# Attention and expert layer on one core: projected tiles, turned heads and the output projection change places between two PSUM banks

## The chip, the cores and the metric

The program runs on one core of a Trainium2 chip. The metric is the device time of one execution in microseconds (us), lower is better. The engines are named as in the profile: PE is TensorE (PEld its weight loads), DVE is VectorE, ACT is ScalarE, POOL is GpSimd, and SP issues most of the DMAs.

## The reference, cut to what matters

```
# x [32, 512, 256]; 16 heads of 16 channels
qk = x @ W_attn + b_attn;  q, k = halves;  v = x
y  = causal_attn(q, k, v)
e  = v[1:] - y[:-1];  k2 = x[:-1] @ W_k2 + b_k2
y2 = causal_attn(q[1:], k2, e), a row of zeros ahead
x  = layernorm(x + y @ W_proj + y2 @ W_proj + 2 * b_proj)
x  = layernorm(x + experts(x))    # eight experts, top 2
```

The arithmetic is float32; the scores come from three products of rounded and rest parts.

## The kernel before

**Units.** One batch element is eight units, called places 0 to 7: places 0 to 3 are the first attention for four groups of four heads, places 4 to 7 the second attention (`a` = 1) for the same groups. 32 batches make 256 units. A unit has ten slots. Every engine walks over the same range of times (unit x 10 + slot) and issues what is due at each; the order on each engine is therefore written out by hand, and engines meet only by semaphores.

**Scores, twice.** In each slot PE makes one bank of transposed scores of the present unit (line 714, into one of three banks `score_t`) and one bank of plain scores of the unit five ahead (`LEAD`, line 725, into one of three banks `score`). ACT takes the exponential of `score_t` (line 570), and POOL masks it on the diagonal (line 456). DVE takes the row maxima of `score` (line 932, two instructions each for most slots); these maxima are transposed on PE (line 793), negated on ACT (lines 604, 605) and sent by DMA into rows of `stack_q`, so that the later score matmul subtracts them. The two matmuls of a slot are issued alternately, and before them PE waits for both:

```
e.wait_ge(s_exp, now - KEY_DEPTH + 1)                             # depth 3
e.wait_ge(s_max, MAX_BEFORE[SLOTS] * u + MAX_BEFORE[n + 1])       # u, n: three slots back
```

So PE can be at most three slots ahead of DVE's maxima.

**Runs and gaps.** PE does the score slots in four runs: slots 0, 1, 2; slots 3, 4; slots 5, 6, 7; slots 8, 9 (`RUNS`). After each run there is a gap with other work:

- First gap (after slot 2): the weighted values of the unit before, key blocks 1, 3, 2 (`weigh`, line 675, into the bank `out_t`). ACT then copies `out_t` to `heads_t` (line 596).
- Second gap (slot 4): in places 1 and 2 the attention sum `y_sum` is transposed into the bank `misc` (line 747) for ACT's copy `y_t` (line 613). In every unit `heads_t` is turned back by four transposes into `out_t` (line 754); DVE divides it by the sums of the softmax (lines 946 and 952, below called the division).
- Third gap (slot 7): in places 7, 0, 1, 2, 4, 5 a projected tile of q, k or k2, six matmuls into `misc` (line 780, `PIECES`), which ACT copies out (`part_f`, line 582) and POOL splits (lines 484, 486). In places 3 and 6 half of the output projection of the batch before, eight matmuls into `misc` (line 810), which DVE adds to the residual (line 960). In places 3 and 7 one transpose of the maxima (line 793).
- Fourth gap (slot 9): the weighted values of key block 0 of this unit, into `out_t` (line 675).

**Following work.** `USUAL` names the unit and slot at which each step of the output projection and the layer norm of a batch is due, counted from the start of the next batch; `LAST` does so for the last batch. DVE's norm statistics (line 319) and the addition (line 960) are issued after the maxima of the slot that is named. POOL makes `value2` or the sum of both attentions (lines 523, 530) at slot 0 two units later. The expert layer starts in the last five units, in which no maxima are left to make, and ends the program.

The change touches the tables above, and the blocks for `ended`, `(place, slot)` and `due(...)` in the programs of all five engines.

Of the kernel before, what the change touches and what calls it, by code (L numbers as in the profile page):

```python
# [14 lines left out]
P = 128  # L15
# [33 lines left out]
PIECES = {(7, 7): ("k", 0, 0), (0, 7): ("q", 0, 1), (1, 7): ("k", 1, 2), (2, 7): ("q", 1, 3),  # L49
          (4, 7): ("k2", 0, 4), (5, 7): ("k2", 1, 5)}  # L50
# [7 lines left out]
USUAL = {"proj": ((3, 7), (6, 7)), "added": ((4, 0), (7, 0)), "stats": ((5, 5), (6, 4), (7, 5), (8, 1)),  # L58
         "var": ((8, 3),), "guess": ((8, 4),), "refine": ((8, 5),), "apply": ((8, 8), (11, 1), (11, 6), (12, 4)), "store": ((12, 7),)}
LAST = {"proj": ((3, 7), (4, 7)), "added": ((3, 9), (4, 9)), "stats": ((4, 1), (4, 3), (5, 1), (5, 2)),  # L60
        "var": ((5, 3),), "guess": ((5, 4),), "refine": ((5, 5),), "apply": ((5, 7), (5, 8), (5, 9), (6, 0)), "store": ((6, 1),)}
# [11 lines left out]
def build_layer(nc, x, x_turned, w_attn, b_qk, w_k2, w_proj, b_proj,  # L73
# [15 lines left out]
    with ctx:  # L89
# [242 lines left out]
        def _(e):  # L332
# [5 lines left out]
            for time in times:  # L338
# [20 lines left out]
                ended = time - 7  # L359
# [12 lines left out]
                if (place, slot) == (5, 5) and 2 <= b < batches:  # L372
# [55 lines left out]
        def _(e):  # L428
# [17 lines left out]
            for time in times:  # L446
# [28 lines left out]
                ended = time - 3  # L475
# [26 lines left out]
                if (place, slot) == (7, 2) and 0 <= ahead + 1 < batches:  # L502
# [12 lines left out]
                if slot == 0 and 0 <= done < end:  # L515
# [38 lines left out]
        def _(e):  # L554
# [4 lines left out]
            for time in times:  # L559
# [24 lines left out]
                ended = time - 7  # L584
# [4 lines left out]

                if slot == 2 and 0 <= unit - 1 < end:  # L590
                    e.wait_ge(s_pv, GROUP * unit)
                    if unit == 1:
                        e.wait_ge(s_floor, GROUP)
                    if unit >= 2:
                        e.wait_ge(s_turned, unit - 1)
                    e.activation(heads_t[:, :], out_t[:, :], ACT.Identity, bias=sum_floor[:, 0:1]).then_inc(s_heads, 1)  # L596
# [9 lines left out]

                for hf in range(halves):
# [53 lines left out]
        def _(e):  # L661
# [17 lines left out]
            for time in times:  # L679
# [56 lines left out]

                b = ahead - 1
                if 0 <= b < batches:
                    for hf in range(halves):
                        if (place, slot) == ((1, 4), (2, 4))[hf]:  # L740
                            e.wait_ge(s_full, min(N_PIECES * (b + 2) + 2 + hf, N_PIECES * batches))
                            if hf == 0:
                                e.wait_ge(s_added, GROUPS * (b + 1))
                            else:
                                e.wait_ge(s_yt, halves * b + 1)
                            for t in range(blocks):
                                done = e.transpose(misc[:, t * P:(t + 1) * P], y_sum[b % 2][:, t, hf * P:(hf + 1) * P], ident[:, :])  # L747
                            done.then_inc(s_yt_pe, 1)


                if slot == 4 and 0 <= unit - 1 < end:
                    e.wait_ge(s_heads, unit)
                    for t in range(blocks):
                        done = e.transpose(out_t[:, t * P:(t + 1) * P], heads_t[:, t * P:(t + 1) * P], ident[:, :])  # L754
                    done.then_inc(s_turned, 1)
# [3 lines left out]
                if piece:  # L759
# [7 lines left out]
                    if place == 1 and ahead >= 1:  # L767
                        e.wait_ge(s_yt, halves * ahead - 1)
                    if place == 2 and ahead >= 1:
                        e.wait_ge(s_yt, halves * ahead)  # L770
                    if place == 4 and ahead >= 1:
                        e.wait_ge(s_attended, 2 * ahead - 1)
                    if place == 7 and ahead + 1 >= 0:
                        e.wait_ge(s_negl, 2 * ahead + 3)
# [9 lines left out]
                for a, b in ((0, ahead + 1), (1, ahead)):  # L784
                    if (place, slot) == ((7, 2), (3, 2))[a] and 0 <= b < batches:
                        e.wait_ge(s_max, MAX_BEFORE[SLOTS] * (UNITS * b + GROUPS * (a + 1)))
                        e.wait_ge(s_full, min(N_PIECES * (b + 1) + (4 if a else 0), N_PIECES * batches))
                        if ahead >= 1:
                            if a:
                                e.wait_ge(s_yt, halves * ahead)  # L790
                            else:
                                e.wait_ge(s_attended, 2 * ahead)
                        e.transpose(misc[0:64, 0:P], max_cols[b % 2][:, a, :, :, :].rearrange("p s h q -> p (s h q)"),
                                    ident[:, :]).then_inc(s_neg_pe, 1)

                now_due = due("proj", time)
                if now_due:
# [4 lines left out]
                    e.wait_ge(s_full, min(N_PIECES * (b + 2) + (6 if pair else 4), N_PIECES * batches))  # L802
                    if pair:
                        e.wait_ge(s_attended, 2 * b + 1)
                    elif b + 1 < batches:
                        e.wait_ge(s_negl, 2 * b + 4)
                    for j in range(2):
                        t = 2 * pair + j
                        for c in range(halves):
                            done = e.matmul(misc[:, j * width:(j + 1) * width], y_t[:, c, t * P:(t + 1) * P], wp[:, c, :],  # L810
                                            start=(c == 0), stop=(c == halves - 1))
                    done.then_inc(s_proj, 1)


                if slot == 9 and 0 <= unit < end:
# [5 lines left out]
                    if unit:  # L821
                        e.wait_ge(s_normal, unit)
# [66 lines left out]
        def _(e):  # L889
# [27 lines left out]
            for time in times:  # L917
# [17 lines left out]
                if slot == 4 and 0 <= unit - 1 < end:  # L935
                    b, a, g = unit_parts(unit - 1)
                    heads = out_t[:, :].rearrange("p (t h w) -> p t h w", t=blocks, h=GROUP)
# [17 lines left out]
                if now_due:  # L955
# [4 lines left out]
                    e.tensor_tensor(rows2, misc[:, :].rearrange("p (t c) -> p t c", t=2), rows2, ALU.add).then_inc(s_attended, 1)  # L960
# [108 lines left out]
```

## Time and profile before

| | |
|---|---|
| median of 3 runs | 2380.05 us (2379.16 to 2387.66) |
| profiled execution, its own time | 2386.96 us |
| its span | 2385.2 us |
| mean granted TensorE clock (share of 2.4 GHz) | 0.991 |
| PE / DVE / ACT / POOL busy | 96% / 87% / 75% / 65% |
| chain that ended last: PE / POOL / ACT | 72% / 12% / 6% |

Busy PE is modelled time of pipelined matmuls. In the timeline a row gives start, length, engine, line, operation, `out<-in` and shapes; an instruction can start before the row ahead of it has ended, so the distance between two starts is what one piece of work costs. "[0.79 <-DVE max_cols L932]" at a row's end is the idle time before it and the instruction that ended it.

### The profile page before, as it was taken

Reading aid. Unit: us, or ns where it says so; the run is one execution under the profiler, and the core shown is the slowest. Engines: PE = TensorE matmul, PEld = TensorE weight load, DVE = VectorE, ACT = ScalarE, POOL = GpSimd, SP = SyncE. Lnnn points to the kernel's source line nnn. Section 1 sums busy time; section 2 is a strip of 40 time slices with the busy share of each in tenths; the row PEclk is TensorE's granted clock in tenths of the full one; section 3 lists DMA queues with packets and bytes.
Section 4 is the critical chain, followed back from the end, with each engine's and each line's share of the span. In section 5 each row is a group of like instructions: output and inputs, shape, how many; then the busy total and the mean of one; then the engine's idle time right before and its main releaser. Section 6 shows DMA issues by size and latency. Waiting matters only on the chain.

```text
span 2385.2 us, 64991 instructions
## 1 busy us (share of the span) xinstructions
PE 2301.7 (96%) x19670; PEld 1325.3 (56%) x19670; DVE 2071.4 (87%) x9178; ACT 1791.5 (75%) x3456; POOL 1553.4 (65%) x2471
## 2 busy tenths in 40 slices
PE   6999999999999999999999999999999999999997
PEld 4555555555555555555555555555555555555454
DVE  5889998998999989999998899998988999998555
ACT  3577777787777778777787787877777777787653
POOL 4466776666767666676776667766666677776342
PEclk9999999999999999999999999999999999999899
DMA  7556555655565565556555655565556556555111
GB/s 121 88 92 104 104 96 98 117 94 99 104 111 103 93 108 108 94 103 110 105 103 97 111 96 105 97 114 103 96 102 109 93 103 109 104 96 95 50 49 58
DMA packets 171909, 235.09 MB, mean 99 GB/s; under 512 B 26280, under 2 KB 87344, under 8 KB 171568
## 3 DMA queue, kind: packets, MB, share of 16 engines
q1 hardware_dynamic: 170608, 229.37, 53.1%
q8 instruction: 166, 2.72, 0.6%
q10 hardware_dynamic: 960, 1.57, 0.5%
q14 instruction: 175, 1.43, 0.3%
HBM read 58.34 MB, written 17.30 MB: 32 GB/s over the span
## 4 chain that ended last, share of the span: by engine, by line
PE 72%; POOL 12%; ACT 6%; issue 5%; DMA 2%; DVE 1%; SPq 1%; ACTq 0%; POOLq 0%; DVEq 0%
PE out_t L675 21%; PE score_t L714 19%; PE misc L780 10%; PE score L725 8%; PE out_t L754 5%; POOL prob L456 4%; PE misc L810 4%; ACT heads_t L596 4%; POOL part_l L486 2%; ACT prob L570 2%; PE score L868 2%; PE misc L747 2%; POOL y_sum L523 1%; DMA stack_q<-neg_l 1%; POOL part_h L484 1%
## 5 line engine op out<-in xcount | busy, mean ns | idle before, releaser
L932 DVE CUSTOM_DVE_ANT_0 junk<-score,mask_rows 128x384 bf16<-128x384 f32 (+3 forms) x3584 | 1679.9, 516 | 197.4 <-PE score L725 190.5
L570 ACT ACTIVATE prob<-score_t 128x512 f32<-128x512 f32 x2560 | 1366.8, 596 | 248.3 <-PE score_t L714 245.2
L456 POOL TENSOR_SCALAR_AFFINE_SELECT prob<-prob 128x512 f32<-128x512 f32 (+1 forms) x1280 | 709.3, 559 | 640.8 <-ACT prob L570 590.3
L714 PE MATMUL score_t<-stack_q,stack_k 50*128 50x128 f32 (+5 forms) x4096 | 973.1, 358 | 10.1 <-DVE max_cols L932 4.5
L725 PE MATMUL score<-stack_k,stack_q 48*128 48x512 f32 (+3 forms) x4096 | 973.2, 348 | 2.5 <-DMA stack_q<-part_l 1.2
L714 PEld LDWEIGHTS score_t<-stack_q,stack_k 50*128 50x128 f32 (+1 forms) x4096 | 610.1, 186 | 540.2 <-ACT prob L570 302.5
L675 PE MATMUL out_t<-prob,value 128*17 128x512 f32 (+3 forms) x8192 | 658.0, 439 | 0.0
L725 PEld LDWEIGHTS score<-stack_k,stack_q 48*128 48x128 f32 x4096 | 616.5, 188 | 24.3 <-DVE max_cols L932 9.3
L932 DVE DVE_READ_ACCUMULATOR2_ANT max_cols<- 128x1 f32 x4096 | 340.5, 83 | 0.0
L675 PEld LDWEIGHTS out_t<-prob,value 128*17 128x17 f32 x8192 | 184.9, 97 | 210.8 <-issue 127.6
L486 POOL TENSOR_TENSOR part_l<-part_f,part_h 128x512 fp32r<-128x512 f32 x192 | 245.5, 1279 | 16.3
L596 ACT ACTIVATE heads_t<-out_t,sum_floor 128x512 f32<-128x512 f32 x256 | 176.4, 689 | 94.9 <-PE out_t L675 94.7
L582 ACT ACTIVATE part_f<-misc,bias_qk 128x512 f32<-128x512 f32 x192 | 132.2, 689 | 138.5 <-PE misc L780 138.5
L754 PE MATMUL out_t<-ident,heads_t 128*128 128x128 f32 x1024 | 164.3, 283 | 11.8 <-ACT heads_t L596 0.8
L932 DVE CUSTOM_DVE_ANT_0 junk<-score,mask_first 128x128 bf16<-128x128 f32 x512 | 146.3, 286 | 0.0
L754 PEld LDWEIGHTS out_t<-ident,heads_t 128*128 128x128 f32 x1024 | 110.9, 141 | 57.7 <-ACT heads_t L596 57.4
L484 POOL CAST part_h<-part_f 128x512 fp32r<-128x512 f32 x192 | 117.7, 613 | 38.0 <-ACT part_f L582 37.4
L780 PE MATMUL misc<-x_t_h,wq_h 128*128 128x512 f32 x256 | 118.1, 461 | 17.7 <-DVE wq_l L906 9.8
L810 PE MATMUL misc<-wp,y_t 128*128 128x256 f32 x512 | 127.2, 391 | 0.0
L780 PE MATMUL misc<-x_t_l,wq_h 128*128 128x512 f32 x256 | 103.7, 405 | 0.0
L810 PEld LDWEIGHTS misc<-wp,y_t 128*128 128x128 f32 x512 | 92.2, 189 | 20.5 <-issue 6.6
L780 PE MATMUL misc<-x_t_h,wq_l 128*128 128x512 f32 x256 | 103.6, 405 | 0.0
(99 smaller groups left out, 1734.3 us busy)
## 6 DMA issues: line engine op xcount, KB each, us to landing
stack_k<-part_h SPq DMA_DIRECT2D x512, 128.0 KB, 4.1
stack_k<-part_l SPq DMA_DIRECT2D x256, 128.0 KB, 5.0
stack_q<-part_h SPq DMA_DIRECT2D x248, 128.0 KB, 4.2
x_full<-x_turned SPq DMA_DIRECT2D x32, 512.0 KB, 13.8
x_in<-L_attn_x SPq DMA_DIRECT2D x32, 512.0 KB, 6.0
layer_out<-x_in SPq DMA_DIRECT2D x32, 512.0 KB, 3.1
stack_q<-part_l SPq DMA_DIRECT2D x124, 128.0 KB, 5.1
x_next<-L_attn_x SPq DMA_DIRECT2D x32, 384.0 KB
```

The costliest lines, as they stand in the source:

```text
L456: e.affine_select(out=view, in_=view, compare_op=ALU.is_ge, fill=0.0, base=-unit_parts(unit)[1], pattern=[[0, runs], [0, cut], [1, P]], ch ...
L484: e.tensor_copy(part_h[i][:, :], part_f[i][:, :]).then_inc(s_split, 1)
L486: e.tensor_tensor(part_l[i][:, :], part_f[i][:, :], part_h[i][:, :].bitcast(F32), ALU.subtract).then_inc(s_split, 1)
L570: e.activation(prob[pair % RING][:, slot % 2 * 512:slot % 2 * 512 + 512], score_t[time % KEY_DEPTH][:, :], ACT.Exp, scale=1.0 / np.sqrt(HE ...
L596: e.activation(heads_t[:, :], out_t[:, :], ACT.Identity, bias=sum_floor[:, 0:1]).then_inc(s_heads, 1)
L675: done = e.matmul(out_t[32 * h:32 * h + HEAD_DIM + 1, first:first + count], value[:, kb, GROUP * g + h, :], prob[pair % RING][:, at:at + c ...
L714: done = e.matmul(score_t[now % KEY_DEPTH][:, col:col + n], keys[rows, pair, kb * P:(kb + 1) * P], stack_q[b % 2][rows, pair, kb * P:token ...
L725: done = e.matmul(score[number % MAX_DEPTH][:, col:col + n], stack_q[b % 2][rows, pair, qb * P:(qb + 1) * P], keys[rows, pair, 0:n], start ...
L754: done = e.transpose(out_t[:, t * P:(t + 1) * P], heads_t[:, t * P:(t + 1) * P], ident[:, :])
L780: done = e.matmul(misc[:, :], w, x_t[px][:, c, :], start=(c == 0 and i == 0), stop=(c == halves - 1 and i == TERMS - 1))
L810: done = e.matmul(misc[:, j * width:(j + 1) * width], y_t[:, c, t * P:(t + 1) * P], wp[:, c, :], start=(c == 0), stop=(c == halves - 1))
L932: e.tensor_tensor_reduce(junk[count % JUNK][:, 0:n], score[number % MAX_DEPTH][:, col:col + n], mask, 1.0, -3e38, ALU.add, ALU.max, max_co ...
```

## The change

Projected tiles move from slot 7 to slot 4, still into `misc`. The transposes of `heads_t` move from slot 4 to slot 7 and go into `misc`, where DVE now reads them, also at slot 7. The transposes of `y_sum` stay in slot 4 but go into `out_t`, behind the projected tile, and the first of them waits for two groups of sums in place of four. The output projection moves from slot 7 to slot 4 and into `out_t`; its addition on DVE moves from slot 0 of the next unit to slot 5 of the same unit, and the norm statistics of a batch to slot 5 of places 4, 5 and 7 and to slot 1 of the next place 0. ACT's copy of a projected tile now stands behind the exponential of slot 4, not of slot 7. The fourth gap waits for ACT's copy of `out_t`, no longer for DVE's division. POOL's split and SP's DMAs of a projected tile keep their places in time; POOL's sums move from slot 0 to slot 2, its copy for `value1` and an x load on SP by two and four slots.

```diff
-PIECES = {(7, 7): ("k", 0, 0), (0, 7): ("q", 0, 1), (1, 7): ("k", 1, 2), (2, 7): ("q", 1, 3),
-          (4, 7): ("k2", 0, 4), (5, 7): ("k2", 1, 5)}
+PIECES = {(7, 4): ("k", 0, 0), (0, 4): ("q", 0, 1), (1, 4): ("k", 1, 2), (2, 4): ("q", 1, 3),
+          (4, 4): ("k2", 0, 4), (5, 4): ("k2", 1, 5)}
...
-USUAL = {"proj": ((3, 7), (6, 7)), "added": ((4, 0), (7, 0)), "stats": ((5, 5), (6, 4), (7, 5), (8, 1)),
-         "var": ((8, 3),), "guess": ((8, 4),), "refine": ((8, 5),), "apply": ((8, 8), (11, 1), (11, 6), (12, 4)), "store": ((12, 7),)}
+USUAL = {"proj": ((3, 4), (6, 4)), "added": ((3, 5), (6, 5)), "stats": ((4, 5), (5, 5), (7, 5), (8, 1)),
+         "var": ((8, 3),), "guess": ((8, 4),), "refine": ((8, 5),), "apply": ((8, 8), (11, 5), (12, 4), (13, 2)), "store": ((13, 4),)}
...
# SP, POOL, ACT: the piece that ended 7, 3, 7 slots ago is now the one that ended 10, 6, 9 ago
-                ended = time - 3
+                ended = time - 6
...
# POOL: the sums
-                if slot == 0 and 0 <= done < end:
+                if slot == 2 and 0 <= done < end:
...
# ACT: heads_t is copied after the negated maxima; y_t comes from out_t
-                        e.activation(y_t[:, hf, :], misc[:, :], ACT.Copy).then_inc(s_yt, 1)
+                        e.activation(y_t[:, hf, :], out_t[:, :], ACT.Copy).then_inc(s_yt, 1)
...
# PE: the transpose of the maxima, now ahead of the projected tile
+                for a, b in ((0, ahead + 1), (1, ahead)):
+                    if (place, slot) == ((7, 2), (3, 2))[a] and 0 <= b < batches:
+                        e.wait_ge(s_max, MAX_BEFORE[SLOTS] * (UNITS * b + GROUPS * (a + 1)))
+                        if unit < 2:
+                            e.wait_ge(s_full, min(N_PIECES * (b + 1) + (4 if a else 0), N_PIECES * batches))
+                        if unit >= 2:
+                            e.wait_ge(s_normal, unit - 1)
...
# PE: transposes of y_sum, behind the projected tile
+                            e.wait_ge(s_heads, min(unit, end))
+                            e.wait_ge(s_added, GROUPS * b + GROUPS // halves * (hf + 1))
...
+                                done = e.transpose(out_t[:, t * P:(t + 1) * P], y_sum[b % 2][:, t, hf * P:(hf + 1) * P], ident[:, :])
...
# PE: output projection
+                    e.wait_ge(s_heads, min(unit, end))
...
+                            done = e.matmul(out_t[:, j * width:(j + 1) * width], y_t[:, c, t * P:(t + 1) * P], wp[:, c, :],
...
# PE: transposes of heads_t, third gap
+                if slot == 7 and 0 <= unit - 1 < end:
+                    e.wait_ge(s_heads, unit)
+                    made = piece_ending(place, 4, ahead, batches)
+                    if made:
+                        e.wait_ge(s_full, made[3] + 1)
...
+                        done = e.transpose(misc[:, t * P:(t + 1) * P], heads_t[:, t * P:(t + 1) * P], ident[:, :])
...
# PE: fourth gap
-                        e.wait_ge(s_normal, unit)
+                        e.wait_ge(s_heads, unit)
+                    if place in (1, 2) and ahead >= 1:
+                        e.wait_ge(s_yt, halves * (ahead - 1) + place)
+                    if place in (3, 6) and ahead >= 1:
+                        e.wait_ge(s_attended, 2 * (ahead - 1) + place // 3)
                     weigh(unit, 0, 0, tokens, start=True)
...
# DVE: the division
-                if slot == 4 and 0 <= unit - 1 < end:
+                if slot == 7 and 0 <= unit - 1 < end:
                     b, a, g = unit_parts(unit - 1)
-                    heads = out_t[:, :].rearrange("p (t h w) -> p t h w", t=blocks, h=GROUP)
+                    heads = misc[:, :].rearrange("p (t h w) -> p t h w", t=blocks, h=GROUP)
```

## Rows read from the trace of the kernel before

**Rows 1.** The page, its first part: busy time and share of each engine.
```profile
PE 2301.7 (96%) x19670; PEld 1325.3 (56%) x19670; DVE 2071.4 (87%) x9178; ACT 1791.5 (75%) x3456; POOL 1553.4 (65%) x2471
```

**Rows 2.** Waits of PE: us in total, times, longest us.
```profile
PEld out_t L754 <- ACT heads_t L596: 57.4, 193, 1.2
...
PE misc L747 <- POOL y_sum L523: 24.0, 30, 0.8
```

**Rows 3.** Timeline of PE, slot 5 of a place 4 to slot 5 of place 5.
```profile
1212.42 0.33 PE L714 MATMUL score_t<-stack_q,stack_k 52*128 52x128 f32 x1
...
1213.56 0.51 PE L780 MATMUL misc<-x_t_h,wk_h 128*128 128x512 f32 x1
...
1215.16 0.38 PE L714 MATMUL score_t<-stack_q,stack_k 52*128 52x256 f32 x1
...
1216.81 0.50 PE L714 MATMUL score_t<-stack_q,stack_k 52*128 52x512 f32 x1
...
1217.77 1.49 PE L675 MATMUL out_t<-prob,value 128*17 128x384 f32 x24
1219.19 0.49 PE L714 MATMUL score_t<-stack_q,stack_k 52*128 52x512 f32 x1
...
1220.07 0.66 PE L754 MATMUL out_t<-ident,heads_t 128*128 128x128 f32 x4
1220.66 0.32 PE L714 MATMUL score_t<-stack_q,stack_k 52*128 52x128 f32 x1
```

**Rows 4.** Timeline of DVE in the same stretch.
```profile
1212.88 0.25 DVE L946 RECIPROCAL rden<-out_t 128x16 f32<-128x16 f32 x1
...
1213.50 0.55 DVE L932 CUSTOM_DVE_ANT_0 junk<-score,mask_rows 128x384 bf16<-128x384 f32 x1
...
1217.11 0.08 DVE L932 DVE_READ_ACCUMULATOR2_ANT max_cols<- 128x1 f32 x1
...
1219.76 0.69 DVE L932 CUSTOM_DVE_ANT_0 junk<-score,mask_rows 128x512 bf16<-128x512 f32 x1 [0.45 <-PE score L725]
...
1222.37 0.42 DVE L319 BATCH_NORM_STATS2 stats<-x_in 128x6 f32<-128x256 f32 x1
```

**Rows 5.** Timeline of PE and DVE in the next unit: last maximum, then the first gap.
```profile
1225.50 0.08 DVE L932 DVE_READ_ACCUMULATOR2_ANT max_cols<- 128x1 f32 x1
...
1226.16 1.49 PE L675 MATMUL out_t<-prob,value 128*17 128x384 f32 x24
```

**Rows 6.** Timeline of PE, second gap of a place 2.
```profile
1262.36 0.50 PE L714 MATMUL score_t<-stack_q,stack_k 50*128 50x512 f32 x1
...
1263.08 0.66 PE L747 MATMUL misc<-ident,y_sum 128*128 128x128 f32 x4
1263.58 0.60 PE L754 MATMUL out_t<-ident,heads_t 128*128 128x128 f32 x4
```

**Rows 7.** Timeline of PE: place 3 of one batch, and of the next.
```profile
1204.99 1.99 PE L810 MATMUL misc<-wp,y_t 128*128 128x256 f32 x8
...
1270.78 0.30 PE L793 MATMUL misc<-ident,max_cols 128*64 128x128 f32 x1
...
1273.57 1.99 PE L810 MATMUL misc<-wp,y_t 128*128 128x256 f32 x8
```

**Rows 8.** Timeline of DVE: the addition and the maximum behind it.
```profile
1278.33 0.69 DVE L960 TENSOR_TENSOR x_in<-misc,x_in 128x512 f32<-128x512 f32 x1
1278.93 0.68 DVE L932 CUSTOM_DVE_ANT_0 junk<-score,mask_rows 128x512 bf16<-128x512 f32 x1
```

**Rows 9.** Timeline of PE, slot 8 of units whose third gap is empty.
```profile
103.36 0.42 PE L714 MATMUL score_t<-stack_q,stack_k 50*128 50x256 f32 x1 [0.79 <-DVE max_cols L932]
...
2213.43 0.35 PE L714 MATMUL score_t<-stack_q,stack_k 50*128 50x256 f32 x1 [0.79 <-DVE max_cols L932]
```

**Rows 10.** Windows: busy us of PE, PEld, DVE, ACT, POOL; granted clock; DMA.
```profile
100.00:110.00 10.00, 9.19 (x65) 4.47 (x68) 7.41 (x34) 6.17 (x13) 5.05 (x10) 0.68 0.48 76
...
1203.00:1271.50 68.50, 67.34 (x609) 38.96 (x606) 62.40 (x282) 54.27 (x107) 47.45 (x77) 1.00 0.58 103
```

More of the change, by code:

```diff
@@ L371, in _ @@
                 b = ahead + 1
-                if (place, slot) == (5, 5) and 2 <= b < batches:
+                if (place, slot) == (5, 9) and 2 <= b < batches:
                     if b >= 3:
@@ L499, in _ @@
                                         ALU.subtract).then_inc(s_xsplit, 1)
-                if (place, slot) == (7, 2) and 0 <= ahead + 1 < batches:
+                if (place, slot) == (7, 4) and 0 <= ahead + 1 < batches:
                     b = ahead + 1
@@ L588, in _ @@
                     fill_stack(e, piece[1], 1)
[L590 to L596, printed above, removed]
                 for a, b in ((0, ahead + 1), (1, ahead)):
@@ L605, in _ @@
                         e.activation(neg_l[:, :].bitcast(F32), misc[0:64, 0:P], ACT.Copy, scale=-1.0).then_inc(s_negh, 1)
+                if slot == 2 and 0 <= unit - 1 < end:
+                    e.wait_ge(s_pv, GROUP * unit)
+                    if unit == 1:
+                        e.wait_ge(s_floor, GROUP)
+                    if unit >= 2:
+                        e.wait_ge(s_turned, unit - 1)
+                    e.activation(heads_t[:, :], out_t[:, :], ACT.Identity, bias=sum_floor[:, 0:1]).then_inc(s_heads, 1)
                 for hf in range(halves):
@@ L734, in _ @@
                     weigh(unit - 1, 2, 2 * P, 2 * P, stop=True)
[L737 to L748, printed above, removed]
-                if slot == 4 and 0 <= unit - 1 < end:
[L752 to L755, printed above, removed]
+                for a, b in ((0, ahead + 1), (1, ahead)):
[3 more added lines that the diff above has]
+                            e.wait_ge(s_full, min(N_PIECES * (b + 1) + (4 if a else 0), N_PIECES * batches))
+                        if unit >= 2:
+                            e.wait_ge(s_normal, unit - 1)
+                        e.transpose(misc[0:64, 0:P], max_cols[b % 2][:, a, :, :, :].rearrange("p s h q -> p (s h q)"),
+                                    ident[:, :]).then_inc(s_neg_pe, 1)
                 piece = piece_ending(place, slot, ahead, batches)
@@ L766, in _ @@
                         e.wait_ge(s_full, n)
[L767 to L774, printed above, removed]
+                    if unit >= 2:
+                        e.wait_ge(s_normal, unit - 1)
+                    if place == UNITS - 1 and ahead + 1 >= 0:
+                        e.wait_ge(s_negh, 2 * ahead + 3)
                     for c in range(halves):
@@ L782, in _ @@
                     done.then_inc(s_piece, 1)
[L784 to L794, printed above, removed]
+                b = ahead - 1
+                if 0 <= b < batches:
+                    for hf in range(halves):
+                        if (place, slot) == ((1, 4), (2, 4))[hf]:
+                            e.wait_ge(s_heads, min(unit, end))
+                            e.wait_ge(s_added, GROUPS * b + GROUPS // halves * (hf + 1))
+                            if hf:
+                                e.wait_ge(s_yt, halves * b + 1)
+                            for t in range(blocks):
+                                done = e.transpose(out_t[:, t * P:(t + 1) * P], y_sum[b % 2][:, t, hf * P:(hf + 1) * P], ident[:, :])
+                            done.then_inc(s_yt_pe, 1)
                 now_due = due("proj", time)
@@ L809, in _ @@
                         for c in range(halves):
-                            done = e.matmul(misc[:, j * width:(j + 1) * width], y_t[:, c, t * P:(t + 1) * P], wp[:, c, :],
+                            done = e.matmul(out_t[:, j * width:(j + 1) * width], y_t[:, c, t * P:(t + 1) * P], wp[:, c, :],
                                             start=(c == 0), stop=(c == halves - 1))
                     done.then_inc(s_proj, 1)
+                if slot == 7 and 0 <= unit - 1 < end:
[3 more added lines that the diff above has]
+                        e.wait_ge(s_full, made[3] + 1)
+                    elif place == 3:
+                        e.wait_ge(s_negh, 2 * ahead + 2)
+                    elif unit >= 2:
+                        e.wait_ge(s_normal, unit - 1)
+                    for t in range(blocks):
+                        done = e.transpose(misc[:, t * P:(t + 1) * P], heads_t[:, t * P:(t + 1) * P], ident[:, :])
+                    done.then_inc(s_turned, 1)
                 if slot == 9 and 0 <= unit < end:
```

14 lines of the change are left out of this document (5 added, 9 removed).

## The prediction

> **What bounds the kernel now.** I read the page's busy times first: PE stands at 96% and DVE at 87% [rows 1], so PE leads, but a DVE with only 13% to spare can become the bound wherever the order of work bunches it. Then I read PE's waits. Two of them are what this change takes on: the turned heads wait for ACT's copy of `out_t`, 57.4 us over 193 units as seen from the weight loads, and the transposes of `y_sum` wait for POOL, 24.0 us, 30 times 0.8 [rows 2]. Together 81 us are the most that could be won, and the first is inflated, since a weight load is issued ahead of the time at which PE could use it.
>
> Last I laid one unit out from the timeline of PE, by the distances between starts [rows 3]. From the first gap (1217.77) to slot 3 it takes 1.42; from slot 3 to the turned heads 0.88; the four transposes 0.59 (1220.07 to 1220.66); slots 5 to 7 take 1.14 (1212.42 to 1213.56); a projected tile 1.60 (to 1215.16); from slot 8 through the fourth gap to slot 0 1.65, and from there to the next first gap 0.96. The sum is 8.24 us.
>
> In a place 2, where the transposes of `y_sum` come in between, the stretch from slot 3 to the gap's first transpose takes only 0.72 [rows 6]. So the wait for the heads costs PE 0.16 in a unit, not 0.3. A whole batch, from the output projection in one place 3 to that in the next, takes 68.58 us [rows 7], which is eight units of 8.24 and 2.7 of extras.
>
> **What DVE does meanwhile.** The code lets PE be three score slots ahead of DVE's maxima at most. From the start of a slot on PE to the start of its maximum on DVE I read 0.57 (slot 3 at 1219.19 [rows 3], maximum at 1219.76 [rows 4]). The maxima of slots 5 to 9 take 3.69 (1213.50 to 1217.19), the division 0.62 (1212.88 to 1213.50) [rows 4]. When PE has to wait for the last maximum, the first gap begins 0.58 after it: its last row ends at 1225.58, the gap begins at 1226.16 [rows 5]. That unit lasted 8.39 from gap to gap, where PE's own sum is 8.24: DVE, with one norm statistic of 0.42 more in it [rows 4], was already late by 0.15.
>
> More telling are the few units whose third gap is empty, in the first and the last batches. With no projected tile there PE stops at slot 8, "[0.79 <-DVE max_cols L932]"; the first and the last of four such stops are shown [rows 9]. The tile in the third gap is what lets DVE work off its three banks.
>
> **The change part by part.**
>
> *Tile out of the third gap, heads and division in.* From the start of slot 5 to the next first gap PE's own work becomes 1.14 + 0.59 (heads) + 1.65 + 0.96 = 4.34 us; before it had 1.60 in place of 0.59. DVE has in the same stretch the maxima of slots 5 to 9, which can't start earlier than slot 5 gives them, and now the division between slots 7 and 8. Since slot 2 of the next unit needs the maximum of slot 9 of this one, the chain is 0.57 + 3.69 + 0.62 + 0.58 = 5.46 us. PE falls short by 1.12 us in every unit and has to wait at slots 1 and 2.
>
> *Tile into the second gap.* In it DVE has at most the maxima of slots 3 and 4 left and then nothing: its spare time moves to where nobody can use it. From the first gap to slot 5 PE takes 1.42 + 0.72 + 1.60 = 3.74, with the heads' wait gone. The new unit is 3.74 + 5.46 = 9.20 us, against 8.24.
>
> *Extras of a batch.* Two transposes of the maxima, 0.3 each [rows 7], together 0.6. The output projection is a row of 1.99 [rows 7] against 1.60 for a tile; I take 0.3 more, twice, so 0.6. It writes `out_t` now, so in places 3 and 6 the wait of 0.16 for the heads stays, 0.3. Transposes of `y_sum` 0.50 each (1263.08 to 1263.58) [rows 6], 1.0. The addition, 0.60 by the distance of two starts [rows 8], stands at slot 5 inside DVE's chain, twice, 1.2. Three of four norm statistics stand there too, 0.42 less the 0.09 by which rows overlap [rows 4, 8], 1.0. The 24.0 us of waits for POOL are gone: the first transposes of `y_sum` need only two groups of sums, long made, and stand behind 1.60 us of tile. Sum: 8 x 9.20 + 4.7 = 78.3 us a batch, 9.7 more than 68.58.
>
> *How often.* Both kinds of scores run together in units 0 to 250, 31.4 batches: 305 us. The ramp before has no exponentials and no division and is bound by the maxima in either order; the expert layer has no maxima. Both are taken as unchanged.
>
> *Costed at nothing.* ACT's copy of a tile moves ahead of the exponentials of slots 5 to 7; slot 8 needs that of slot 5. ACT is busy 1791.5 us [rows 1], 7.0 a unit, and PE waits for DVE later in the same unit, which covers it. Were that cover gone, an ACT late by a tenth would cost 25 us over 251 units. POOL's and SP's parts of a tile keep their times; POOL's sums move by two slots, and `value2` of a group is wanted about two units later. The fourth gap no longer waits for the division, but it never was the last thing in. The third gap's transposes wait for ACT's copy of the tile, which has the 1.14 of slots 5 to 7 to be done.
>
> *The sum.* 2387 us of the profiled execution + 305 = 2692. That execution stands 7 us above the median, so about 2685 for the median; I say 2690, with two or three drops of the clock (below) in it.
>
> *Bounds.* The uncertain terms are the two joins, 0.57 and 0.58. With both at nothing DVE's chain is 4.31, as long as PE's own 4.34, and the stall is gone; each row I have shows them at their full size, so I take that. A tenth less on each is 50 us less in all.
>
> **Rivals.**
>
> *Faster: DVE keeps pace.* The change then gives what it removes: 24 us of waits for POOL, and 0.16 in the four units of a batch (places 7, 0, 4, 5) that at most had the heads' wait and lose it, 20 us. That is 2336. Every bank would have to be free in time, so DVE's chain would have to be 1.12 us shorter than its rows. The four stops of 0.79 speak against it. The Trainium skill, "Perfetto Trace Analysis", section "Matmuls", says that independent matmul groups should rotate through PSUM banks, so that evacuation of one overlaps the next. By that rule the change is right and the time is this rival's; the trace agrees for `out_t` and `misc`, but the rule leaves out the three `score` banks.
>
> *A smaller loss.* DVE's chain is right, but half of the joins is hidden in the new order: a unit of 8.63, 73.7 a batch, +161 us, 2541.
>
> *The clock falls as well.* The first stop of 0.79 stands in a stretch of 10 us with a granted clock of 0.68, so some 6.4 us at 1.2 GHz [rows 10], 3.2 us of PE's work, of which the stall takes up some: say 2.5 a drop. Against it: in the middle batch the clock is 1.00 throughout [rows 10], with a wait of 0.8 in it. The new stalls are 1.1 us long in each unit, 1.4 to 1.7 with an addition or a statistic. If only the two units of a batch with an addition bring a drop, 63 drops cost 157 us: 2849. If all five units with extras do, 3080. The Trainium skill, "TensorE: Matmul & The Clock Gate", section "A second HAM failure mode: psum-queue depth-cycling", tells of a kernel that paused briefly between groups as it cycled through PSUM banks, and whose clock went back and forth. By that rule this rival would be the likeliest; the middle batch's 1.00 in spite of a wait speaks against it, the first stop for it.
>
> *No change:* gain and stall would have to cancel, at a stall of some 0.17 a unit; nothing points there.
>
> **How the numbers follow.** My forecast (2580 to 2790 by itself) 0.65; the clock falls as well 0.15; a smaller loss 0.10; faster 0.08; no change 0.02. About 0.5%, 12 us, is what a measurement of this kernel tells from none. So: slower 0.90, same 0.02, faster 0.08. The range reaches from 2500, most of the smaller loss, to 2900, the clock's rival with additions alone.
>
> **What would show each step.** Of the stall: PE's waits before `score_t` and `score` for `max_cols` L932 at slots 1 and 2, in sum about 1.1 us a unit, 280 us in all, where DVE shows no idle time from slot 5 to slot 9. Of the second gap: DVE idle for about a microsecond before the maximum of slot 5. Of the removed waits: none of `y_sum` for POOL, and the turned heads with no wait for ACT. Of the unit: 9.2 us from first gap to first gap in place 4 or 5 plus 0.33 for the statistic; 78 us from one place 3 to the next. The prediction is wrong if PE meets slot 2 with the maximum of slot 9 already made, or if the granted clock in the middle of the run is well below 1.00.

## The result and the profile after

| | before | after |
|---|---|---|
| median | 2380.61 us (2379.16 to 2387.66, 4 runs) | 2665.5 us (2661.09 to 2667.76, 4 runs) |
| span of the profiled execution | 2385.2 us | 2662.8 us |
| granted TensorE clock | 0.991 | 0.990 |

The ratio is 1.119, 95% interval 1.116 to 1.122: the change costs 285 us. Predicted were 2690, in a range of 2500 to 2900.

The first part of the page of the kernel after:

```profile
PE 2434.9 (91%) x19670; PEld 1361.6 (51%) x19670; DVE 2056.3 (77%) x9178; ACT 1824.1 (69%) x3456; POOL 1566.9 (59%) x2471
```

Against [rows 1] no engine has more instructions, and yet PE shows 133 us more busy time for the same 19670 matmuls. Busy time counts matmuls that overlap only once, and a PE that is held up between them overlaps them less. The 1024 plain score matmuls of 512 columns are an example: 411.2 us busy before, 510.8 after, while the mean row grew only from 473 to 503 ns, which is 31 us of the 100. So the wait view alone understates the loss. PE's waits, in us, times, longest:

```profile
PE score_t L714 <- ACT prob L570: 72.4, 275, 0.7
PE score_t L714 <- DVE max_cols L934: 54.8, 131, 0.7
PE out_t L794 <- ACT heads_t L605: 14.7, 31, 0.7
```

They add up to 142 us, half of the 285, and the first line names ACT at stops that in truth last until DVE is done, as shown below for one of them. The wait of the `y_sum` transposes for POOL [rows 2] is gone.

Now one unit, from the first gap of place 4 to that of place 5, in the timeline of PE:

```profile
1200.70 1.49 PE L675 MATMUL out_t<-prob,value 128*17 128x384 f32 x24
...
1202.84 0.50 PE L765 MATMUL misc<-x_t_h,wk_h 128*128 128x512 f32 x1
...
1204.43 0.32 PE L714 MATMUL score_t<-stack_q,stack_k 52*128 52x128 f32 x1
...
1205.49 0.66 PE L809 MATMUL misc<-ident,heads_t 128*128 128x128 f32 x4
...
1206.99 0.35 PE L714 MATMUL score_t<-stack_q,stack_k 52*128 52x256 f32 x1 [0.23 <-DVE max_cols L934]
...
1209.70 0.47 PE L714 MATMUL score_t<-stack_q,stack_k 52*128 52x512 f32 x1 [0.19 <-ACT prob L570]
1210.13 1.49 PE L675 MATMUL out_t<-prob,value 128*17 128x384 f32 x24
```

and DVE in the same unit:

```profile
1205.05 0.56 DVE L934 CUSTOM_DVE_ANT_0 junk<-score,mask_rows 128x384 bf16<-128x384 f32 x1 [0.97 <-PE score L725]
...
1205.74 0.42 DVE L319 BATCH_NORM_STATS2 stats<-x_in 128x6 f32<-128x256 f32 x1
...
1207.47 0.25 DVE L948 RECIPROCAL rden<-misc 128x16 f32<-128x16 f32 x1
...
1209.13 0.42 DVE L934 CUSTOM_DVE_ANT_0 junk<-score,mask_rows 128x256 bf16<-128x256 f32 x1
1209.47 0.08 DVE L934 DVE_READ_ACCUMULATOR2_ANT max_cols<- 128x1 f32 x1
1209.47 0.69 DVE L934 CUSTOM_DVE_ANT_0 junk<-score,mask_rows 128x512 bf16<-128x512 f32 x1
```

The unit reads as the prediction's chain. PE takes 3.73 from the first gap to slot 5 (1200.70 to 1204.43). DVE, idle for 0.97 before it, starts the maximum of slot 5 0.62 later, then has no idle time until the maximum of slot 9 ends at 1209.55: 4.50. The next first gap starts 0.58 behind that. 3.73 + 0.62 + 4.50 + 0.58 = 9.43.

The row at 1209.70 names ACT. In the timeline of ACT, the exponentials of this unit are:

```profile
1205.62 2.54 ACT L570 ACTIVATE prob<-score_t 128x512 f32<-128x512 f32 x5
...
1209.00 1.11 ACT L570 ACTIVATE prob<-score_t 128x512 f32<-128x512 f32 x2 [0.85 <-PE score_t L714]
```

The run of five ended at 1208.16, ACT was idle for 0.85, and of the next two the first ended half way, at about 1209.55. The code lets slot 2 wait only for the exponential of slot 9, which is three slots back and the last of the five: ready 1.5 us before PE went on. DVE's maximum of slot 9 ended at 1209.55, 0.15 before it. PE waits for both semaphores, and the view puts such a wait down to an event near its end; DVE was what it waited for. The run with the fast DVE below confirms that; place 0 is the exception, as after_division9 shows.

The windows over one batch, from place 3 to the next (busy PE, PEld, DVE, ACT, POOL; granted clock; DMA):

```profile
1192.83:1270.80 77.97, 71.99 (x606) 40.26 (x606) 61.82 (x283) 55.39 (x107) 47.82 (x77) 1.00 0.52 91
```

Against the middle batch before [rows 10] the batch is 9.5 us longer. The clock is 1.00 in both, and DVE, ACT and POOL have the same work to within 1.2 us.

Where the 277.6 us between the two spans lie is read from the output projections of place 3, the first and the last of the 30 that follow each other at equal distances. Before:

```profile
174.62 1.99 PE L810 MATMUL misc<-wp,y_t 128*128 128x256 f32 x8
...
2167.72 1.99 PE L810 MATMUL misc<-wp,y_t 128*128 128x256 f32 x8
```

and after:

```profile
178.96 1.97 PE L794 MATMUL out_t<-wp,y_t 128*128 128x256 f32 x8 [0.47 <-ACT heads_t L605]
...
1192.83 1.97 PE L794 MATMUL out_t<-wp,y_t 128*128 128x256 f32 x8 [0.47 <-ACT heads_t L605]
...
1270.93 1.97 PE L794 MATMUL out_t<-wp,y_t 128*128 128x256 f32 x8 [0.47 <-ACT heads_t L605]
...
2441.32 1.97 PE L794 MATMUL out_t<-wp,y_t 128*128 128x256 f32 x8 [0.47 <-ACT heads_t L605]
```

Ahead of the first the new kernel has lost 4.3 us, behind the last 4.0. Between them stand 29 batches of 78.01 against 68.73 us: 269.3 us.

### The profile page after: what moved, and what is told of

Its sections match the earlier page's. It is cut to its first block, busy times and chain, and to the rows that moved or that the text cites. A ratio compares the mean times of both kernels' runs of the same rounds, so it can differ in the third digit from the quotient of the medians.

```text
span 2662.8 us, 65370 instructions
## 1 busy us (share of the span) xinstructions
PE 2434.9 (91%) x19670; PEld 1361.6 (51%) x19670; DVE 2056.3 (77%) x9178; ACT 1824.1 (69%) x3456; POOL 1566.9 (59%) x2471
## 4 chain that ended last, share of the span: by engine, by line
PE 70%; ACT 11%; DVE 8%; issue 7%; POOL 3%; DMA 1%; ACTq 0%; SPq 0%; POOLq 0%; DVEq 0%
PE out_t L675 22%; PE score_t L714 22%; PE misc L765 12%; ACT prob L570 8%; PE out_t L794 5%; DVE junk L934 4%; PE score L725 4%; PE misc L809 2%; PE score L870 2%; DVE stats L319 1%; DVE max_cols L934 1%; PE out_t L779 1%; ACT part_f L582 1%; ACT heads_t L605 1%; PE score L886 1%
## 5 line engine op out<-in xcount | busy, mean ns | idle before, releaser
L570 ACT ACTIVATE prob<-score_t 128x512 f32<-128x512 f32 x2560 | 1390.9, 598 | 387.6 <-PE score_t L714 370.7
L714 PE MATMUL score_t<-stack_q,stack_k 50*128 50x128 f32 (+5 forms) x4096 | 1101.2, 367 | 168.0 <-ACT prob L570 72.4
L725 PE MATMUL score<-stack_k,stack_q 48*128 48x512 f32 (+3 forms) x4096 | 1108.7, 356 | 4.7 <-DVE max_cols L934 3.1
L714 PEld LDWEIGHTS score_t<-stack_q,stack_k 50*128 50x128 f32 (+1 forms) x4096 | 635.3, 185 | 790.4 <-ACT prob L570 446.6
L725 PEld LDWEIGHTS score<-stack_k,stack_q 48*128 48x128 f32 x4096 | 642.4, 187 | 27.4 <-DVE max_cols L934 11.9
L809 PE MATMUL misc<-ident,heads_t 128*128 128x128 f32 x1024 | 167.6, 286 | 0.0
L794 PE MATMUL out_t<-wp,y_t 128*128 128x256 f32 x512 | 125.5, 388 | 18.7 <-ACT heads_t L605 14.7
L809 PEld LDWEIGHTS misc<-ident,heads_t 128*128 128x128 f32 x1024 | 107.6, 141 | 47.5 <-issue 47.4
L794 PEld LDWEIGHTS out_t<-wp,y_t 128*128 128x128 f32 x512 | 92.3, 189 | 43.6 <-issue 33.5
```

The lines of the kernel that those rows point to most:

```text
L570: e.activation(prob[pair % RING][:, slot % 2 * 512:slot % 2 * 512 + 512], score_t[time % KEY_DEPTH][:, :], ACT.Exp, scale=1.0 / np.sqrt(HE ...
L714: done = e.matmul(score_t[now % KEY_DEPTH][:, col:col + n], keys[rows, pair, kb * P:(kb + 1) * P], stack_q[b % 2][rows, pair, kb * P:token ...
L725: done = e.matmul(score[number % MAX_DEPTH][:, col:col + n], stack_q[b % 2][rows, pair, qb * P:(qb + 1) * P], keys[rows, pair, 0:n], start ...
L794: done = e.matmul(out_t[:, j * width:(j + 1) * width], y_t[:, c, t * P:(t + 1) * P], wp[:, c, :], start=(c == 0), stop=(c == halves - 1))
L809: done = e.transpose(misc[:, t * P:(t + 1) * P], heads_t[:, t * P:(t + 1) * P], ident[:, :])
```

## The experiments

Each kernel ran beside the kernel before on the same chip; ratios are to that. The length of a unit is the distance from one first gap to the next, as the median over some 30 batches of the profiled execution.

### after_division9: the division taken out of DVE's chain

The transposes of the heads stay in the third gap; DVE divides only at slot 9, behind the maxima of slots 8 and 9.

```diff
-                if slot == 7 and 0 <= unit - 1 < end:
+                if slot == 9 and 0 <= unit - 1 < end:
```

> The changed kernel with one part moved: DVE's division (reciprocal and product, 0.62 us) is issued after the maxima of slot 9, not of slot 7. Theory A (DVE's chain from slot 5 to slot 9 stops PE at slots 1 and 2): the division leaves the chain and falls into DVE's idle time before slot 3; 0.62 a unit, 251 units, 156 us less than the changed kernel, about 2510. Theory B (ACT's copy of the tile, now ahead of the exponentials of slots 5 to 7, stops PE): no change from 2665. Theory C (the exchange of the banks costs, by the waits it brought to misc and out_t): no gain, rather a loss, since the next writer of misc waits longer for the division: 2665 or more.

Measured: 2533.6 us (2532.58 to 2535.95), ratio 1.064 (1.062 to 1.066). The unit of place 4 fell from 9.43 to 8.83, by the length of the division, and so did those of places 1 to 3 and 5 to 7, within 0.02. Place 0 stayed: 9.26 and now 9.25. So 132 us of the 285 are back, where 156 were expected. PE's wait for DVE is still there:

```profile
PE score_t L714 <- DVE max_cols L934: 53.3, 125, 0.7
```

So DVE's chain sets seven of the eight units, the division is one link of it, and more than half of the loss has nothing to do with the division. Place 0 is set by ACT. In the kernel after, its end reads:

```profile
1169.21 0.60 ACT L289 ACTIVATE x_in<-x_in,shift,rstd 128x256 f32<-128x256 f32 x1 [0.88 <-POOL shift L277]
1169.72 0.58 ACT L570 ACTIVATE prob<-score_t 128x512 f32<-128x512 f32 x1
...
1169.99 0.08 DVE L934 DVE_READ_ACCUMULATOR2_ANT max_cols<- 128x1 f32 x1
...
1170.35 0.50 PE L714 MATMUL score_t<-stack_q,stack_k 50*128 50x512 f32 x1 [0.32 <-ACT prob L570]
```

A step of the layer norm waits for POOL, the exponential of slot 9 behind it ends at 1170.30, and DVE's maximum of slot 9 had been done at 1170.07.

### before_division7: the same link put into the kernel before

```diff
-                if slot == 4 and 0 <= unit - 1 < end:      # DVE's division
+                if slot == 7 and 0 <= unit - 1 < end:
```

> The kernel before with DVE's division alone moved from behind the maxima of slot 4 to behind those of slot 7; transposes, tiles and banks stay. Theory A: DVE's chain from slot 5 to the first gap becomes 5.46, PE's own path there is 1.14 + 1.60 + 2.61 = 5.35 with the tile still in the third gap, so the stall is 0.1 a unit, 28 us, and some more with statistics: 2400 to 2420. If the division's place and not the tile's were the main cause: above 2500.

Measured: 2413.48 us (2412.97 to 2414.28), ratio 1.013 (1.011 to 1.015), 31 us. The same 0.6 us of DVE's work in the same slots costs a quarter of what it does in the new kernel, since the tile in the third gap lets DVE catch up.

### before_tile45: two tiles a batch moved to the second gap, nothing else

```diff
-          (4, 7): ("k2", 0, 4), (5, 7): ("k2", 1, 5)}
+          (4, 4): ("k2", 0, 4), (5, 4): ("k2", 1, 5)}
...
-                ended = time - 3
+                ended = time - (6 if (time - 6) // SLOTS % UNITS in (4, 5) else 3)      # POOL; SP: 10 for 7
```

> The kernel before with the projected tiles of places 4 and 5 alone moved to the second gap, behind the turned heads; banks, division, the other tiles, POOL's split and SP's DMAs as they were. Theory A: in these two units the third gap is empty, PE's own work from slot 5 to the first gap is 3.75 and DVE's chain 4.84, so each is 1.1 us longer, of 256 units 63: 69 us, about 2450, with stops at slots 8 and 9 for max_cols. Theory B: ACT's copy moves ahead of exponentials here too; at the size of 285 us in 192 tiles, 1.5 us each, 94 us, but with stops for ACT. Theory C: no bank is exchanged, so 2380.

Measured: 2455.54 us (2452.12 to 2465.74), ratio 1.031 (1.028 to 1.033). In the profiled execution, the one of 2465.74, the unit of place 4 grew from 8.24 to 9.07. That of place 5 grew from 8.39 to 9.37 in only eight batches; in 22 others it took 10.3 to 10.7. With heads and division still in slot 4, PE stops in the empty third gap of place 5:

```profile
1193.38 0.35 PE L714 MATMUL score_t<-stack_q,stack_k 52*128 52x256 f32 x1 [0.42 <-DVE max_cols L932]
...
1194.40 0.35 PE L714 MATMUL score_t<-stack_q,stack_k 52*128 52x256 f32 x1 [0.51 <-DVE max_cols L932]
```

All 30 units have these two stops, the second of 0.51 or 0.52. What differs is the clock over the 6 us from 6 us behind the first gap on: 0.72 in each of the 22 long ones, 1.00 in each of the eight others. One of either kind (last columns: granted clock, DMA share, GB/s):

```profile
1123.12:1129.12 6.00, 5.40 (x55) 2.49 (x55) 5.35 (x24) 4.26 (x9) 4.50 (x7) 1.00 0.87 164
1193.56:1199.56 6.00, 5.49 (x46) 2.06 (x45) 4.72 (x23) 3.19 (x7) 4.47 (x7) 0.72 0.78 156
```

The move of the tile is enough by itself: DVE's chain adds 0.83 and 0.98, 1.8 a batch and some 55 us in all, where 1.1 a unit and 69 us were expected. The lower clock does the rest: the profiled span is 78.8 us longer than that of the kernel before, and 22 units longer by some 1.2 make 26 of them. That the total came near 69 is luck. In the other three executions, whose mean clock was 0.974 to 0.981 against 0.968, only the total is known.

In place 4 the view names ACT for a first stop of 0.69 at slot 8, and rightly: DVE's maximum of slot 5 was done at 1184.16, and PE went on at 1184.58, behind ACT's exponential of slot 5, which stood behind the copy of the tile. This delay is covered. DVE has no idle time from 1183.38 to 1186.98, the end of its maximum of slot 9, and the next first gap starts 0.58 behind that.

### before_short and after_short: DVE made fast in both kernels

Each maximum reads 128 columns in place of up to 512. The true row maxima are not formed; everything else is there.

```diff
+                        n = P
+                        mask = mask_rows[a][:, 0:n]
                         e.tensor_tensor_reduce(...
```

> The kernel before, with every maximum taken over 128 columns only (work left out: the true row maxima are not formed, all else runs), so that DVE has about 3.4 us of maxima in a unit where it had 6.7. Theory A: DVE was late by 0.15 in a few units only, and in the empty third gaps; 2360 to 2375. Theories B and C say nothing else.

> The changed kernel with the same short maxima. Theory A: DVE's chain shrinks to about 3.9 us, under PE's own 4.34; the stall is gone and what is left is what the change removed, 24 us of waits for the sums and some 0.16 in four units of a batch: 25 to 45 us less than the kernel before with short maxima, about 2325. Theory B: ACT's order is unchanged, so most of the 285 us stays: above 2550. Theory C: the same, above 2550.

Measured: before_short 2341.31 us (2338.38 to 2341.89), ratio 0.983 (0.981 to 0.985); after_short 2389.68 us (2386.68 to 2391.7), ratio 1.004 (1.002 to 1.005). With a fast DVE the difference between the two orders shrinks from 285 us to 48. DVE is confirmed as what PE waited for, against the line that names ACT, in all places but 0, whose unit takes 9.24 with the fast DVE and 9.26 without. before_short came out 19 us under its expected range: DVE had held more units of the kernel before than its few visible stops told, place 4 by 0.15 (8.24 to 8.09), place 5 by 0.27, place 7 by 0.41. But 48 us of loss stay where the expectation had the new order ahead: its time is missed by some 65 us, so something else was in the new order, behind DVE. The timeline of after_short in a place 0 shows it:

```profile
1108.46 0.69 ACT L582 ACTIVATE part_f<-misc,bias_qk 128x512 f32<-128x512 f32 x1 [0.62 <-PE misc L765]
...
1109.39 2.04 ACT L570 ACTIVATE prob<-score_t 128x512 f32<-128x512 f32 x4
...
1112.31 0.60 ACT L289 ACTIVATE x_in<-x_in,shift,rstd 128x256 f32<-128x256 f32 x1 [0.89 <-POOL shift L277]
1112.82 2.04 ACT L570 ACTIVATE prob<-score_t 128x512 f32<-128x512 f32 x4
...
1113.45 0.49 PE L714 MATMUL score_t<-stack_q,stack_k 50*128 50x512 f32 x1 [0.79 <-ACT prob L570]
```

ACT's row L289, part of the layer norm, stands in its order between the exponentials of slots 8 and 9 and waits 0.89 for POOL. Slot 2 of PE waits for the exponential of slot 9. A second stop, in place 3, is the output projection's:

```profile
1133.53 1.97 PE L794 MATMUL out_t<-wp,y_t 128*128 128x256 f32 x8 [0.46 <-ACT heads_t L605]
```

Here it is ACT's copy `heads_t` that is late: it now stands behind the two copies of the negated maxima. Over the run the two kinds of stop are

```profile
PE score_t L714 <- ACT prob L570: 32.2, 87, 0.8
...
PE out_t L794 <- ACT heads_t L605: 14.6, 31, 0.7
```

### after_short_act and after_short_act2: ACT's order mended, with the fast DVE

The first issues the guess of the layer norm ahead of the tile's copy, and `heads_t` ahead of the negated maxima in both places; as in after_short, the true row maxima are not formed. The second keeps the negated maxima first in place 7, and moves the part of the layer norm behind the exponential of slot 9:

```diff
-          ... "refine": ((8, 5),), "apply": ((8, 8), (11, 5), (12, 4), (13, 2)), ...
+          ... "refine": ((8, 5),), "apply": ((9, 1), (11, 5), (12, 4), (13, 2)), ...
```

> The changed kernel with short maxima (128 columns each, true row maxima not formed) and ACT's order mended in two places: the guess of the norm's root stands ahead of the copy of a projected tile, and the copy of heads_t ahead of the negated maxima again. Theory A2 (what is left of the loss once DVE is fast, 2390 against 2341 with short maxima, is ACT's order: in place 0 the guess waits behind the tile's copy and with it POOL's refinement and the exponential of slot 9, 0.79; in place 3 the output projection waits for heads_t behind the negated maxima, 0.46): 1.2 a batch of 31, 35 to 40 us less, about 2353. Rival (the waits brought by the exchange of banks): 2390, no change.

> The changed kernel with short maxima (true row maxima not formed), with two repairs of ACT's order: in place 3 the copy of heads_t ahead of the negated maxima (in place 7 behind, as in the change), and the first application of the norm, which in place 0 stands between the exponentials of slots 8 and 9 and waits for POOL, due at slot 1 of the next unit. If ACT's order is what is left of the loss: 0.5 of place 3 and 0.79 of place 0, 31 times, 40 us less than after_short, about 2350. If the wait only moves on: 2385.

Measured: after_short_act 2385.29 us (2383.68 to 2390.46), ratio 1.002 (1.001 to 1.003), not distinct from after_short: place 3 won 0.5 (9.46 to 8.96), place 7 lost 0.36 (8.41 to 8.77), and place 0 kept its stop (9.24 to 9.19), because POOL's part was as late as before: POOL does it behind its mask of slot 5, whose exponential stands behind the tile's copy in either order. My expectation of 2353 was wrong in that. after_short_act2: 2348.32 us (2347.43 to 2350.04), ratio 0.986 (0.984 to 0.988). Place 0 fell to 8.20, place 3 to 8.95. PE's waits of this kernel, the one for `prob` down from 32.2:

```profile
PE score_t L723 <- ACT prob L570: 9.6, 59, 0.4
```

So 41 of the 48 us were these two entries in ACT's order, and the new arrangement is 7 us from before_short, still no faster, though it no longer pays the 24 us of waits for POOL. Against before_short it wins 0.77 in place 1 and 0.25 in place 0, and loses 0.36, 0.26, 0.47 and 0.19 in places 3, 4, 6 and 7. In a place 4 PE starts slot 8 0.77 behind the turned heads, where four transposes take 0.59, and then takes 0.92 to the fourth gap, where before_short takes 0.67. It waits for ACT's exponentials of slots 5 and 6, which begin only behind the copy of the tile and a step of the norm. What places 3, 6 and 7 lose was not tried.

### before_early_sums, before_early_stats, before_lead_in: what of the change is worth keeping

The first takes one thing from the change, the wait for two groups of sums in place of four. The second moves DVE's norm statistics from slots 4 and 5 to slot 2 as well. The third adds to the first one of a tile's six matmuls in the second gap, to cover the wait for the heads.

```diff
-                            if hf == 0:
-                                e.wait_ge(s_added, GROUPS * (b + 1))
-                            else:
+                            e.wait_ge(s_added, GROUPS * b + GROUPS // halves * (hf + 1))
+                            if hf:
                                 e.wait_ge(s_yt, halves * b + 1)
...
# before_early_stats, further
+         "stats": ((5, 2), (6, 2), (7, 2), (8, 1))
...
# before_lead_in, further: slot 4 of places 0, 4, 5; the same matmul is left out at slot 7
+                    e.matmul(misc[:, :], w, x_t[PARTS_Q[0]][:, 0, :], start=True, stop=False)
```

> The kernel before with one wait eased as in the change: the transposes of the first half of y_sum wait for two groups of sums, those of the second for four. The 24.0 us of PE's waits for POOL (30 times 0.8) go: 0.65 to 0.8 of each place 1, 20 to 24 us, about 2359. If they were hidden behind something later in the batch: 2381.

> As before_early_sums, and three of the four norm statistics of a batch moved on DVE from slots 5, 4 and 5 of places 5, 6 and 7 to slot 2, where DVE idles before slot 3. Theory A: the statistic in DVE's chain cost 0.15 in place 5 and 0.27 in place 7; 13 us less than before_early_sums, about 2346. If DVE's chain did not bind in those units before: the same as before_early_sums.

> before_early_sums and one matmul of six of the projected tiles of places 0, 4 and 5 taken from the third gap into the second, ahead of the turned heads (0.23 to 0.33 us of PE's work while ACT copies heads_t). Theory A: the wait of 0.16 for heads_t in these three units is covered, 15 us less than before_early_sums, about 2340, as long as DVE's chain (0.57 + 3.69 + 0.58 = 4.84 from slot 5, the division done ahead of it) stays under PE's 5.35 - 0.25 = 5.10. If the division, late by the same 0.1 to 0.3, pushes the chain: no gain, 2355, with waits for max_cols at slots 1 and 2.

Measured: 2354.75 us (2352.56 to 2357.72), ratio 0.988 (0.987 to 0.990); 2353.38 (2352.25 to 2353.45), 0.988 (0.986 to 0.989); 2350.71 (2347.74 to 2354.68), 0.987 (0.985 to 0.989). The early sums are worth 1.2%, 28 us: the line of [rows 2] for POOL's `y_sum` is gone from the waits of that kernel. The other two aren't told apart from it. The statistics gave place 5 0.20 (8.39 to 8.19) and place 7 0.05 (8.62 to 8.57), but place 0 lost 0.11 (8.37 to 8.48), where the expectation had 13 us in all; the matmul, for which 15 us were expected, gave 0.1 in place 4 and nothing in places 5 and 0. In place 5 the bound is DVE's maxima, since it fell to 8.12 with the fast DVE, and cover for PE's wait alone buys nothing there; what sets the 8.37 of place 0, which with the fast DVE took 8.45, stays open. All three beat both kernels.

## Why the prediction was right, point by point

**The mechanism.** The step on which all rests, that DVE's maxima of slots 5 to 9 with the division and two joins make a chain longer than PE's work between slot 5 and the first gap, is shown: by the unit above; by the division, whose removal shortens seven of eight units by its own length; by the tile alone, which reproduces the loss in two places; and by the fast DVE, which takes away 237 of 285 us. PE's own work was put a little too high: with the fast DVE the unit of 8.24 takes 8.09, so 0.15 of it was DVE's already.

**The size of a unit.** Forecast for place 4 were 9.20 + 0.33 = 9.53, measured 9.43. The term that was mis-sized is the block of maxima, division and statistic: 3.69 + 0.62 + 0.33 = 4.64 against 4.50, since the 3.69 of [rows 4] still held a little idle time, and a read of 0.08 that the next maximum did not overlap. The first join was 0.62 for 0.57, the second 0.58 as said, the stretch to slot 5 3.73 for 3.74.

**The extras of a batch.** A plain unit, 9.43 less the statistic's 0.34, is 9.09. Over it places 1 and 2 have 0.48 each (`y_sum` 0.50 forecast), places 4 and 5 0.34 (statistic, 0.33), place 7 0.62 (0.63), place 6 1.14 (addition, projection and heads 1.06). Place 3 has 1.69 for 1.36: the wait for the heads is 0.47 there, not 0.16, because the copy stands behind the negated maxima, of which the prediction took no account. (The transposes of the maxima stand at slot 2, in the first gap, and not in the third as the section on the kernel before has it; that is why they meet the heads.) Place 0 has 0.17 that the prediction didn't have: there ACT, not DVE, is the last to be done, as after_division9 shows. In sum 5.3 for 4.7, and a batch of 78.0 for 78.3: the unit forecast too long and the extras too short offset each other, which is luck.

**How often.** This is the largest miss: 31.4 batches of 9.7 were forecast, 305 us; 29 of 9.28 came, 269 us, and only 8 us more from everything around them. At either end some units got shorter: the place 7 ahead of the last batch took 8.62 for 10.22, and in the last batch place 0 took 8.43 for 9.23 and place 3 10.26 for 11.19. The kernel before had stopped there for its maxima, in the empty third gaps, but the four stops of 0.79 [rows 9] are only 3 us of the difference; the rest was not taken apart.

**Costed at nothing.** ACT's moved copies cost little here only because DVE covers them, the condition that the prediction named, in all places but 0 and 3. The bound of 25 us for a cover that is gone was too low: two entries alone measured 41 us (2389.68 less 2348.32), and 9.6 us of waits for `prob` are left.

**The rivals.** *Faster* fell twice: DVE keeps no pace, and where it is made to (after_short, 2390 against 2341) the order of ACT eats the gain; with that mended the two orders tie at 2341 and 2348. Of the gain it counted on, 24.0 us for POOL are real (28 measured alone), while the 20 us of the heads' wait are seen in one of four places: place 0 takes 8.45 in before_short, with that wait, and 8.20 in after_short_act2, without it, but place 5 takes 8.12 in both, and places 4 and 7 are longer. The wait for POOL went by the eased semaphore alone, since before_early_sums loses it with every bank as before. Moving the turned heads to `misc` did remove their weight loads' wait for ACT: the line of 57.4 us [rows 2] has no counterpart in the kernel after. That agrees with the Trainium skill ("Perfetto Trace Analysis", "Matmuls"), which has independent matmul groups rotate through PSUM banks. The three `score` banks decided all the same. *A smaller loss* fell, both joins stand at full size. *The clock falls as well* did not come: 1.00 in the batch above.

**Left open.** What places 3, 6 and 7 of the new order lose once DVE is fast was not tried. Nor was the whole new order run with DVE's chain shortened and the true maxima kept.

## What to carry to other kernels

Before moving filler work on the bound engine, ask which other engine uses that stretch to catch up, and add up that engine's chain from the first slot to the one that waits for it, joins included: a mean share of 87% busy says nothing about it. A stall in the few units where the filler is absent anyway is the experiment already made for you. The order on a follower engine (here ACT) should be counted too, even where it is covered: it is the next bound. And take the useful part of a change alone; one relaxed wait was worth 28 us by itself, and the change with it cost 285.

## What the runs showed of the hardware

The prediction gave 0.15 to a clock that falls with the stops. In the kernel after, a place 6 has PE's stops of 0.69, 0.24 and 0.19 within 3.3 us, and over 15 us around them the granted clock stays at 1.00, the 2.4 GHz level:

```profile
1226.64 0.35 PE L714 MATMUL score_t<-stack_q,stack_k 52*128 52x256 f32 x1 [0.69 <-ACT prob L570]
...
1228.80 0.47 PE L714 MATMUL score_t<-stack_q,stack_k 52*128 52x512 f32 x1 [0.24 <-DVE max_cols L934]
1229.49 0.46 PE L714 MATMUL score_t<-stack_q,stack_k 52*128 52x512 f32 x1 [0.19 <-DVE max_cols L934]
```

```profile
1221.00:1226.00 5.00, 4.82 (x38) 3.50 (x34) 2.96 (x12) 3.24 (x6) 3.20 (x5) 1.00 1.09 185
1226.00:1231.00 5.00, 3.92 (x38) 1.66 (x42) 4.92 (x23) 2.99 (x5) 3.53 (x5) 1.00 0.36 51
```

In before_tile45 the two stops of place 5, 0.42 and 0.51, are shorter in sum (0.93 against 1.12), and yet behind them the clock was 0.72 over 6 us in 22 of 30 batches. At levels of 1.2 and 2.4 GHz this is 3.4 us at the lower one, and it made the unit 0.9 to 1.3 us longer. In the eight other batches the same two stops left it at 1.00. The Trainium skill ("TensorE: Matmul & The Clock Gate", "A second HAM failure mode: psum-queue depth-cycling") tells of short pauses that make the clock go back and forth: the trace of before_tile45 agrees, that of the kernel after does not. The length of the stops doesn't tell the two apart, and what does these runs don't show.

Held-up matmuls showed as busy time: 133 us more busy PE for the same 19670 instructions, by longer rows and by less overlap. Distances between starts of the same row in two units gave the loss where busy and idle times each gave a part.
